# Projection and attention as one unrolled stage, by blocks of 512 queries

## The chip, the core and the metric

The kernel runs on one NeuronCore of a Trainium2 chip. The metric is device time in microseconds, the median of several executions. A profiled execution also gives the span from its first to its last instruction and a record of every instruction and DMA.

## What is computed

A transformer layer on 2 batches of 2048 tokens, width 256: a modulated layer norm, causal attention with 16 heads of 16 whose scores have three parts, and a feed-forward with 8 experts of which each token uses 2. Cut to what matters here:

```python
h = layernorm(x) * (1 + ca) + sa
q, k, v = split_heads(h @ qkv_w.T)                    # 16 heads of 16
scores = alpha * tanh(q k^T / beta)
soft, hexc = tanh(h @ hex_w.T), tanh(h @ q6_w.T)      # 6 codes each
scores += lam / 2 * soft soft^T                       # the same for all heads
scores += hexc M_head hexc^T / 6 * scale              # M_head is 6 x 6
out = softmax(causal(scores)) @ v
x = x + ga * (out @ out_w.T)
# then a layer norm, a router (top 2 of 8) and the experts; the change leaves these alone
```

## The kernel before

Five stages run one after the other, each with its own block of instruction streams for TensorE (PE), ScalarE (ACT), VectorE (DVE), GpSimd (POOL) and the DMA queue of SyncE (SP). No engine enters a stage before all have left the one before.

`stage_modulation` (L166) loads x whole, takes the statistics of its rows, computes the modulation rows, and ACT normalises x in place (L226 to L228).

`stage_projection` (L321) loops over eight blocks of 512 tokens. For each, POOL applies scale and shift (L431, L436), PE transposes the four tiles (L449) and multiplies: codes (L455), q and k in four groups of 128 rows (L461), the bilinear term (L466), v (L470), and a bound called guard (L476, L477). q, k, codes and bilinear term are split into two fp32r halves whose sum is the fp32 value; ACT and DVE do that. SP writes it all to scratch tensors in DRAM, with 23 DMAs a block (L392 to L415).

`stage_attention` (L550) loops over eight iterations, one for each batch and group of four heads. An iteration has 36 steps in a fixed order: for query block `qb` (0 to 3) of 512 queries, 4·qb full steps of 128 keys by 512 queries, then three diagonal steps, the last of which is 256 wide. A step has four parts. PE makes the raw scores of four heads (`raw_scores`, L669) in four PSUM banks that are not doubled, so it waits for the tanh of the step before. PE makes the bilinear scores of the four heads one after the other in two banks (`bilinear`, L681); each head waits for the sum of the head two before. PE multiplies the weights by v (`weighted_values`, L696). ACT does tanh (L734) and exp (L741), DVE the four sums (L771) and at the end of a query block the copy of the output (L779). POOL masks diagonal tiles (L654). PE runs raw scores three steps ahead: at step s it issues raw(s+3), bilinear(s+2) of heads 2 and 3, values(s), bilinear(s+3) of heads 0 and 1. All stationary operands of raw and bilinear scores have 128 rows, half of them zeros against the other head. Seven iterations are one loop body, the eighth is written out behind it. Loads (`load_block`, L581, 15 DMAs for each 512 keys) go into single buffers and wait until the iteration before has used them. With the first loads goes the load of x for the next stage (L625).

`stage_output` (L812) projects, adds x and takes statistics for 32 tiles; then come the router and the experts.

The lines that set the order on PE, and what SP does in the loop:

```python
for s in range(NSTEP):
    raw_scores(*at(s + PE_LEAD))
    bilinear(*at(s + PE_LEAD - 1), LAST_TWO)
    weighted_values(it, s)
    bilinear(*at(s + PE_LEAD), FIRST_TWO)
...
for qb in range(NBLK):
    if qb == NBLK - 1 and not last:
        for c in range(NBLK):
            load_block(sp, it + 1, c)
    store_out(sp, it, qb)
```

## Time and profile before

| | |
|---|---|
| time, median of 3 runs | 2195.11 us (2193.89 to 2205.54) |
| span of the profiled execution | 2187.8 us |
| PE busy / weight loads | 1909.5 us (87%) / 1097.2 us |
| ACT busy | 1282.9 us (59%) |
| DVE busy | 1300.8 us (59%) |
| POOL busy | 357.6 us (16%) |
| DMA | 172.28 MB in 139177 packets |

The profile is read by stage: busy shares of the whole span mix stages with different limits. In the timeline a row is a run of instructions of one kind: start, time from the first start to the last end, engine, line, tiles, count, and in brackets how long the engine was idle before it and what ended that. Ends of matmuls are modelled, and two ACT instructions in a row overlap in the records by some 0.15 us, so the distance from start to start is what one costs.

### The profile page before, as it was taken

Reading aid. Unit: us, or ns where it says so; the run is one execution under the profiler, and the core shown is the slowest. Engines: PE = TensorE matmul, PEld = TensorE weight load, DVE = VectorE, ACT = ScalarE, POOL = GpSimd, SP = SyncE. Lnnn points to the kernel's source line nnn. Section 1 sums busy time; section 2 is a strip of 40 time slices with the busy share of each in tenths; the row PEclk is TensorE's granted clock in tenths of the full one; section 3 lists DMA queues with packets and bytes.
Section 4 is the critical chain, followed back from the end, with each engine's and each line's share of the span. In section 5 each row is a group of like instructions: output and inputs, shape, how many; then the busy total and the mean of one; then the engine's idle time right before and its main releaser. Section 6 shows DMA issues by size and latency. Waiting matters only on the chain. (4 is left out here: it accounts for less than half of the span.)

```text
span 2187.8 us, 35435 instructions
## 1 busy us (share of the span) xinstructions
PE 1909.5 (87%) x9314; PEld 1097.2 (50%) x9315; DVE 1300.8 (59%) x2620; ACT 1282.9 (59%) x1387; POOL 357.6 (16%) x383
## 2 busy tenths in 40 slices
PE   2988199898999999989799996699089999999998
PEld 1433044444444444444344445588056667776665
DVE  5543177676877777777577774765234444444443
ACT  4323099898998989989799992244012222222222
POOL 1330200100001000000000003215501111111111
PEclk7988599999999999999899998899589999999999
DMA  3455661506033060521605204622262112222211
GB/s 122 153 171 199 152 152 43 107 10 125 23 71 82 19 130 5 101 52 40 108 5 101 53 6 127 200 116 79 89 190 34 32 31 34 34 34 34 34 31 25
DMA packets 139177, 172.28 MB, mean 79 GB/s; under 512 B 16672, under 2 KB 89248, under 8 KB 138976
## 3 DMA queue, kind: packets, MB, share of 16 engines
q1 hardware_dynamic: 116672, 143.00, 26.6%
q0 software_dynamic: 13824, 19.03, 5.0%
q10 hardware_dynamic: 8608, 9.47, 1.3%
q8 instruction: 22, 0.36, 0.1%
q14 instruction: 51, 0.42, 0.1%
HBM read 106.42 MB, written 65.03 MB: 78 GB/s over the span
## 5 line engine op out<-in xcount | busy, mean ns | idle before, releaser
L771 DVE SCALAR_TENSOR_TENSOR probs<-probs,scal,bil_ps 128x512 f32<-128x512 f32 (+1 forms) x1152 | 773.6, 715 | 278.5 <-ACT probs L734 169.6
L734 ACT ACTIVATE probs<-raw_ps 128x2048 f32<-128x2048 f32 (+1 forms) x288 | 518.7, 1801 | 84.3 <-PE raw_ps L669 84.3
L741 ACT ACTIVATE probs<-probs 128x2048 f32<-128x2048 f32 (+1 forms) x288 | 529.7, 1839 | 34.8 <-DVE probs L771 34.8
L681 PE MATMUL bil_ps<-u_mv,w_st 128*128 128x512 f32 (+3 forms) x1280 | 469.9, 426 | 54.1 <-DVE probs L771 30.8
L1442 ACT ACTIVATE hid_t<-h_tr_ps,b 128x128 f32<-128x128 f32 x576 | 156.3, 383 | 475.7 <-PE h_tr_ps L1406 409.6
L681 PEld LDWEIGHTS bil_ps<-u_mv,w_st 128*128 128x128 f32 x1280 | 217.3, 192 | 410.5 <-DVE probs L771 380.8
L669 PE MATMUL raw_ps<-q_mv,k_st 128*128 128x512 f32 (+3 forms) x1280 | 337.1, 390 | 52.8 <-DMA v_sb<-v_rows 45.1
L696 PE MATMUL o_ps<-probs,v_sb 128*32 128x512 f32 (+3 forms) x2560 | 298.5, 548 | 0.5 <-POOL probs L654 0.5
L669 PEld LDWEIGHTS raw_ps<-q_mv,k_st 128*128 128x128 f32 x1280 | 212.3, 194 | 143.9 <-ACT probs L734 70.1
L1397 PE MATMUL fc_ps<-w,rows_t 128*128 x576 | 262.1, 598 | 1.2 <-issue 0.6
L1417 PE MATMUL fc_ps<-w,hid_t 128*128 x1152 | 260.9, 380 | 1.7 <-DMA b<-in_b 0.9
L654 POOL TENSOR_SCALAR_AFFINE_SELECT probs<-probs 128x512 f32<-128x512 f32 x128 | 79.7, 635 | 982.5 <-ACT probs L741 982.5
L1417 PEld LDWEIGHTS fc_ps<-w,hid_t 128*128 128x128 f32 x1152 | 213.6, 190 | 28.2 <-issue 2.5
L1366 POOL DMA_INDIRECT out<-y,token x72 | 112.1, 1557 | 495.4 <-DVE y L1485 481.8
L1397 PEld LDWEIGHTS fc_ps<-w,rows_t 128*128 128x128 f32 x576 | 105.2, 193 | 107.0 <-issue 106.9
L1472 DVE COPY hid<-fc_ps 128x1024 f32<-128x1024 f32 x72 | 88.1, 1224 | 114.7 <-PE fc_ps L1397 114.7
L1481 DVE TENSOR_TENSOR y<-fc_ps,b 128x256 f32<-128x256 f32 x72 | 30.6, 424 | 204.7 <-PE fc_ps L1417 204.7
L696 PEld LDWEIGHTS o_ps<-probs,v_sb 128*32 128x32 f32 x2560 | 52.8, 109 | 66.9 <-ACT probs L741 36.4
L1406 PEld LDWEIGHTS h_tr_ps<-ident,hid 128*128 128x128 f32 x576 | 67.4, 141 | 37.5 <-issue 37.4
L1151 POOL DMA_INDIRECT x_rows<-rows_sb,place x64 | 62.6, 978 | 105.1 <-DVE place L1184 87.7
L1133 ACT ACTIVATE act_t<-hid_ps,rb 128x512 f32<-128x512 f32 x64 | 44.0, 689 | 60.7 <-PE hid_ps L1104 60.5
L1406 PE MATMUL h_tr_ps<-ident,hid 128*128 128x128 f32 x576 | 74.7, 273 | 0.0
(186 smaller groups left out, 1313.7 us busy)
## 6 DMA issues: line engine op xcount, KB each, us to landing
q_mv<-q_split SPq DMA_DIRECT2D x128, 128.0 KB
rows<-x_rows SPq DMA_DIRECT2D x72, 130.0 KB, 2.1
v_rows<-v_st SPq DMA_DIRECT2D x8, 1024.0 KB, 5.2
k_st<-k_split SPq DMA_DIRECT2D x64, 128.0 KB
k_st<-k_split SPq DMA_DIRECT2D x128, 64.0 KB
v_sb<-v_rows SPq DMA_DIRECT2D x32, 256.0 KB
o_t<-o_sb SPq DMA_DIRECT2D x32, 256.0 KB, 2.2
o_t_sb<-o_t SPq DMA_DIRECT2D x32, 256.0 KB, 2.8
```

Source lines behind the costliest of these rows:

```text
L669: mm = pe.matmul(raw_ps[:, hd, column:column + width], k_st[:, hd // 2, kt * P:(kt + 1) * P], q_mv[:, hd, qb * BLK + query:qb * BLK + quer ...
L681: mm = pe.matmul(bil_ps[:, hd % 2, column:column + width], w_st[:, kt * P:(kt + 1) * P], u_mv[:, hd, qb * BLK + query:qb * BLK + query + w ...
L696: mm = pe.matmul(o_ps[hd * VW:(hd + 1) * VW, query:query + width], v_sb[:, kt, hd * VW:(hd + 1) * VW], probs[:, s % NBUF, hd, column:colum ...
L734: act.activation(probs[:, s % NBUF, :, first:BLK], raw_ps[:, :, first:BLK], ACT.Tanh).then_inc(tanh_ready, 1)
L741: act.activation(scores, scores, ACT.Exp).then_inc(exp_ready, 1)
L771: dve.scalar_tensor_tensor(scores, scores, scal[:, ALPHA:ALPHA + 1], bil_ps[:, hd % 2, first:BLK], ALU.mult, ALU.add).then_inc(sum_ready, 1)
L1366: pool.indirect_dma_start(out, bass.IndirectOffsetOnAxis(ap=token[:, u:u + 1], axis=0), y[:, u % 2, :], None, compute_op=ALU.add).then_inc ...
L1397: mm = pe.matmul(fc1_ps[:, half * BLK:(half + 1) * BLK], rows_t[:, p, k * P:(k + 1) * P], w1[:, ds(e * (KC * HID) + (k * HID + half * BLK) ...
L1406: tr = pe.transpose(h_tr_ps[:, hc * P:(hc + 1) * P], hid[:, p, hc * P:(hc + 1) * P], ident[:, :])
L1417: mm = pe.matmul(fc2_ps[:, 0:D], hid_t[:, p, hc * P:(hc + 1) * P], w2[:, ds(e * (HC * D) + hc * D, D)], start=(hc == 0), stop=(hc == HC - 1))
L1442: silu = act.activation(hid_t[:, p, cols], h_tr_ps[:, cols], ACT.Silu, bias=b1[:, ds(e * HC + hc, 1)])
L1472: dve.tensor_copy(hid[:, p, :], fc1_ps[:, :]).then_inc(hid_ready, 1)
```

## The change

Projection and attention become one stage, `stage_front`, without loops. The unit of order is a block of 512 queries of one batch; the eight blocks come as (batch 0, queries 0), (batch 1, queries 0), (batch 0, queries 1) and so on, each with four iterations for the four groups of heads. So there are 32 iterations of 3, 7, 11 or 15 steps and 288 steps as before. Keys, queries, bilinear operands and values of an iteration have two buffers each; an iteration loads the keys and values of all query blocks up to its own.

The projection of a block is cut into eleven parts: two transposes (T0, T1), codes (C), q and k (Q0 to Q3), bilinear term (L), v (V0, V1), guard (G). Blocks 0 and 1 are projected ahead of attention (all but G of block 1), with five PSUM banks in turn. For the six others one part stands behind `weighted_values` in each of eleven steps in a row, beginning where block i−2 begins its attention; these parts use one bank, `part_ps`. DVE empties that bank between heads 1 and 2 of its sums one step later; POOL splits three steps later, after that step's mask; SP stores four steps later. The halves of q and k, codes and bilinear term come from POOL instead of ACT and DVE (for blocks 0 and 1 those of q and k still come from ACT and DVE).

ACT no longer normalises all of x; x is loaded again by blocks, and DVE (block 0 and 1) or POOL normalises it. Raw and bilinear scores use stationary operands of 64 and 50 rows, heads 0 and 2 in the lower half of the array's rows, heads 1 and 3 in the upper half. The load of x for `stage_output` moves to that stage, ahead of its first loads of `o_t`.

```diff
+assert TPB == 4
+BLOCKS = [(i % B, i // B) for i in range(N_BLK)]
+ITERS = [(i, g) for i in range(N_BLK) for g in range(NG)]
...
+STEPS = [(it, pieces) for it, (i, _) in enumerate(ITERS) for pieces in block_steps(BLOCKS[i][1])]
 NSTEP = len(STEPS)
-LAST_OF = {qb: max(s for s, (q, _) in enumerate(STEPS) if q == qb) for qb in range(NBLK)}
-FIRST_OF = {qb: min(s for s, (q, _) in enumerate(STEPS) if q == qb) for qb in range(NBLK)}
...
+DIAG = [s for it in range(len(ITERS)) for s in range(LAST[it] - 2, LAST[it] + 1)]
+MASKS_BEFORE = {s: n for n, s in enumerate(DIAG)}
...
+PARTS = ["T0", "T1", "C", "Q0", "L", "Q1", "Q2", "V0", "Q3", "V1", "G"]
+EARLY = 2
+START = {i: FIRST[i * NG] for i in range(N_BLK)}
+HEAD_PARTS = ([(0, o) for o in PARTS[:-1]] + [(1, o) for o in ("T0", "T1", "C")] + [(0, "G")]
+              + [(1, o) for o in PARTS[3:-1]])
+SLOT = {START[0]: (1, "G")}
+SLOT.update({START[i - EARLY] + (i == EARLY) + n: (i, o) for i in range(EARLY, N_BLK) for n, o in enumerate(PARTS)})
+PART_ORDER = HEAD_PARTS + [SLOT[s] for s in sorted(SLOT)]
+PART_NUMBER = {part: n for n, part in enumerate(PART_ORDER)}
+EMPTIED = {part: sum(o != "C" for _, o in PART_ORDER[:n + 1]) for n, part in enumerate(PART_ORDER)}
+POOL_LAG = 3
+NORM_AT = {START[i - EARLY - 1] + 4 + 2 * t: (i, t) for i in range(EARLY + 1, N_BLK) for t in range(TPB)}
+STORE_AT = {s + POOL_LAG + 1: part for s, part in SLOT.items()}
+KEYS_AT = {max(LAST[it - 2] - PE_LEAD, 0): it for it in range(2, len(ITERS))}
+BIAS_AT = {LAST[it - 2] - PE_LEAD + 1: it for it in range(2, len(ITERS))}
+VALUES_AT = {LAST[it - 2] + 1: it for it in range(2, len(ITERS))}
+CODES_AT = {LAST[i * NG - 2] - PE_LEAD - 1: i for i in range(1, N_BLK)}
+ROWS_AT = {FIRST[(i - EARLY - 2) * NG + 2]: i for i in range(EARLY + 2, N_BLK)}
...
-            stage_modulation(nc, a, modrow, ident, scal, x_sb, stats, rstd, lattice)
-            stage_projection(nc, a, dram, modrow, ident, scal, x_sb, lattice)
+            stage_modulation(nc, a, modrow, ident, scal, shift, rstd, lattice)
+            stage_front(nc, a, dram, modrow, ident, scal, shift, rstd, lattice)
...
-            act.wait_ge(shift_ready, 1)
-            for n in range(NTILE):
-                tile = x_sb[:, n * D:(n + 1) * D]
-                act.activation(tile, tile, ACT.Identity, bias=shift[:, n:n + 1], scale=rstd[:, n:n + 1])
...
+        k_st = sb("k_st", [P, 2, HG // 2, T], F32R)
+        q_mv = sb("q_mv", [P, 2, HG // 2, BLK], F32R)
+        w_st = sb("w_st", [P, B, T], F32R)
+        u_mv = sb("u_mv", [P, 2, HG // 2, BLK], F32R)
+        v_sb = sb("v_sb", [P, 2, T // P, HG * VW])
+        probs = sb("probs", [P, NBUF, HG, BLK])
+        o_sb = sb("o_sb", [P, 2, BLK])
...
+        part_ps = ps("part_ps", [P, BLK])
...
+            def load_keys(it):
+                i, g = ITERS[it]
+                c, p = BLOCKS[i][1], it % 2
+                if it >= 2:
+                    sp.wait_ge(raw_mm, LAST[it - 2] + 1)
+                for m in range(2):
+                    sp.wait_ge(st_qk[m], 32 * N_QK * (i + 1))
+                seen, own = slice(0, (c + 1) * BLK), slice(c * BLK, (c + 1) * BLK)
+                k_both = heads("k_split", 2 * HD, i, g, seen).rearrange("(j z r) t -> z r j t", z=2, r=2 * HD)
+                q_rows = heads("q_split", 2 * HD, i, g, own).rearrange("(j z r) t -> z r j t", z=2, r=2 * HD)
+                load = lambda dst, src: sp.dma_start(dst.bitcast(F32), src).then_inc(keys_in[p], 16)
+                for z in range(2):
+                    row = z * ROWS
+                    load(k_st[row:row + 2 * HD, p, :, seen], k_both[z])
+                    load(k_st[row + 2 * HD:row + 3 * HD, p, :, seen], k_rows[z, 1])
+                    load(k_st[row + 3 * HD:row + 4 * HD, p, :, seen], k_rows[z, 0])
+                    for half in range(2):
+                        load(q_mv[row + half * 2 * HD:row + (half + 1) * 2 * HD, p, :, :], q_rows[z])
...
+            load_rows(0)
+            load_rows(1)
+            for o in PARTS[:-1]:
+                store(0, o)
+            load_keys(0)
+            sp.wait_ge(pad_ready, 1)
+            load_codes(0)
+            load_values(0)
+            load_rows(2)
+            store(0, "G")
+            load_bias(0)
+            load_keys(1)
+            load_bias(1)
+            load_values(1)
+            load_rows(3)
+            for o in PARTS[:-1]:
+                store(1, o)
+            for s in range(NSTEP):
+                if s in CODES_AT:
+                    load_codes(CODES_AT[s])
+                if s in KEYS_AT:
+                    load_keys(KEYS_AT[s])
+                if s in BIAS_AT:
+                    load_bias(BIAS_AT[s])
+                if s in VALUES_AT:
+                    load_values(VALUES_AT[s])
+                if s in STORE_AT:
+                    store(*STORE_AT[s])
+                if s in ROWS_AT:
+                    load_rows(ROWS_AT[s])
+                if s - 1 in LAST:
+                    store_out(LAST.index(s - 1))
+            store_out(len(ITERS) - 1)
...
+            def split_heads(i, m):
+                pool.wait_ge(emptied, EMPTIED[i, f"Q{m}"])
+                pool.wait_ge(st_qk[m % 2], 16 * N_QK * (2 * i + m // 2))
+                then_wait(pool.tensor_copy(qk_hi[:, m % 2, :], qk_f[:, m % 2, :]))
+                pool.tensor_tensor(qk_lo[:, m % 2, :], qk_f[:, m % 2, :], qk_hi[:, m % 2, :].bitcast(F32),
+                                   ALU.subtract).then_inc(lo_ready, 1)
+                pool.wait_ge(lo_ready, 4 * (i - EARLY) + m + 1)
...
+            for s in range(NSTEP):
+                if s in MASKS_BEFORE:
+                    mask(s)
+                if s - POOL_LAG in SLOT:
+                    i, o = SLOT[s - POOL_LAG]
+                    if o == "C":
+                        split_codes(i)
+                    elif o == "L":
+                        split_lattice(i)
+                    elif o == "G":
+                        split_guard(i)
+                    elif o[0] == "Q":
+                        split_heads(i, int(o[1]))
+                if s in NORM_AT:
+                    normalise(pool, then_wait, *NORM_AT[s])
...
+            def project(i, o):
+                bank = bank_of((i, o))
+                emptied_before(pe, (i, o))
+                if o[0] == "T":
+                    k = int(o[1])
+                    for t in range(TPB):
+                        pe.wait_ge(h_ready, TPB * i + t + 1)
+                        mm = pe.transpose(bank[:, t * P:(t + 1) * P], h[:, t, k * P:(k + 1) * P], ident[:, :])
+                elif o == "C":
+                    pe.wait_ge(emptied, EMPTIED[i, "T1"])
+                    for k in range(KC):
+                        mm = pe.matmul(bank[0:HROWS, :], wcode[:, k, :], h_t[:, k, :],
+                                       start=(k == 0), stop=(k == KC - 1))
+                elif o[0] == "Q":
+                    m = int(o[1])
+                    for k in range(KC):
+                        mm = pe.matmul(bank, wqkv[:, k, m * P:(m + 1) * P], h_t[:, k, :],
...
+                        row = hd % 2 * ROWS
                         mm = pe.matmul(raw_ps[:, hd, column:column + width],
-                                       k_st[:, hd // 2, kt * P:(kt + 1) * P],
-                                       q_mv[:, hd, qb * BLK + query:qb * BLK + query + width],
-                                       start=True, stop=True)
...
+                for hd in pair:
+                    row = hd % 2 * ROWS
+                    if HG * s + hd >= 2:
+                        pe.wait_ge(sum_ready, HG * s + hd - 1)
                     for kt, column, query, width in pieces:
-                        mm = pe.matmul(bil_ps[:, hd % 2, column:column + width], w_st[:, kt * P:(kt + 1) * P],
-                                       u_mv[:, hd, qb * BLK + query:qb * BLK + query + width],
+                        mm = pe.matmul(bil_ps[:, hd % 2, column:column + width],
+                                       w_st[row:row + BIAS_ROWS, b, kt * P:(kt + 1) * P],
+                                       u_mv[row:row + BIAS_ROWS, p, hd // 2, query:query + width],
                                        start=True, stop=True)
...
+            pe.wait_ge(p_in, 64)
+            for i, o in HEAD_PARTS:
+                project(i, o)
+            pe.wait_ge(emptied, EMPTIED[HEAD_PARTS[-1]])
...
+            for s in range(NSTEP):
+                if s + PE_LEAD < NSTEP:
+                    raw_scores(s + PE_LEAD)
+                if s + PE_LEAD - 1 < NSTEP:
+                    bilinear(s + PE_LEAD - 1, LAST_TWO)
+                weighted_values(s)
+                if s in SLOT:
+                    project(*SLOT[s])
+                if s + PE_LEAD < NSTEP:
+                    bilinear(s + PE_LEAD, FIRST_TWO)
...
+                if s - 2 in SLOT and SLOT[s - 2][1] == "C":
+                    make_codes(SLOT[s - 2][0])
+                exp(s)
...
+            for t in range(TPB):
+                normalise(dve, then_wait, 0, t)
+            dve.memset(w_st[:, :, :].bitcast(F32), 1.0).then_inc(pad_ready, 1)
+            dve.memset(v_st[:, :, :, HD:VW], 1.0).then_inc(ones_ready, 1)
+            for n, (i, o) in enumerate(HEAD_PARTS):
+                if o != "C":
+                    empty(i, o)
+                if i == 0 and o[0] == "Q":
+                    normalise(dve, then_wait, 1, int(o[1]))
...
+            for s in range(NSTEP):
+                for hd in range(HG):
+                    if hd == HG // 2 and s - 1 in SLOT and SLOT[s - 1][1] != "C":
+                        empty(*SLOT[s - 1])
+                    if s + DVE_LEAD < NSTEP:
+                        score_sum(s + DVE_LEAD, hd)
+                if s in LAST:
+                    evacuate(LAST.index(s))
...
             sp.dma_start(token_f[:, :], a["token_rows"]).then_inc(t_in, 16)
+            sp.dma_start(rows_sb[:, :].rearrange("p (n d) -> p n d", d=PAY)[:, :, 0:D],
+                         a["x"].rearrange("(n p) d -> p n d", p=P)).then_inc(x_back, 16)
             for m in range(OB):
```

## Rows read from the trace of the kernel before

**Rows 1.** Busy time by stage: us and count of PE, PEld, DVE, ACT, POOL; clock, DMA share, GB/s

```profile
0.00:44.40 44.40, 12.28 (x24) 5.14 (x25) 30.30 (x123) 20.66 (x41) 0.20 (x4) 0.84 0.39 132
44.40:244.30 199.90, 148.14 (x400) 63.64 (x400) 82.83 (x113) 56.12 (x80) 51.45 (x64) 0.84 0.50 170
...
268.00:1321.00 1053.00, 990.78 (x5116) 477.81 (x5115) 791.35 (x1183) 982.10 (x576) 79.70 (x128) 0.97 0.32 65
```

**Rows 2.** Timeline of SP in projection: first issue of two blocks in a row

```profile
173.81 0.75 SPq L392 DMA_DIRECT2D code_split<-w_hi  x1
...
196.28 0.74 SPq L392 DMA_DIRECT2D code_split<-w_hi  x1
```

**Rows 3.** Timeline of one full step of attention

```profile
901.68 2.81 DVE L771 SCALAR_TENSOR_TENSOR probs<-probs,scal,bil_ps 128x512 f32<-128x512 f32 x4 [0.76 <-ACT probs L734]
...
903.14 0.19 PEld L681 LDWEIGHTS bil_ps<-u_mv,w_st 128*128 128x128 f32 x1 [0.47 <-DVE probs L771]
903.20 1.93 ACT L734 ACTIVATE probs<-raw_ps 128x2048 f32<-128x2048 f32 x1
...
903.57 1.07 PE L696 MATMUL o_ps<-probs,v_sb 128*32 128x512 f32 x8
...
906.76 1.94 ACT L734 ACTIVATE probs<-raw_ps 128x2048 f32<-128x2048 f32 x1
```

**Rows 4.** Groups by form in attention: busy us, mean ns, idle before

```profile
L734 ACT ACTIVATE probs<-raw_ps 128x1024 f32<-128x1024 f32 x32 | 34.0, 1063 | 0.0
```

**Rows 5.** Timeline at returns of the loop: first return, then the sixth

```profile
412.35 1.06 ACT L741 ACTIVATE probs<-probs 128x1024 f32<-128x1024 f32 x1 [3.85 <-DVE probs L771]
...
1068.14 0.88 DVE L771 SCALAR_TENSOR_TENSOR probs<-probs,scal,bil_ps 128x256 f32<-128x256 f32 x2 [6.21 <-issue]
...
1084.80 1.88 ACT L734 ACTIVATE probs<-raw_ps 128x2048 f32<-128x2048 f32 x1 [2.04 <-PE raw_ps L669]
```

**Rows 6.** Timeline: end of modulation, a memset, the first tanh

```profile
38.78 0.42 DVE L317 SCALAR_TENSOR_TENSOR modrow<-gate_sign,gate_abs 128x256 f32<-128x256 f32 x1
...
247.09 1.76 DVE L761 MEMSET w_st<- 64x2048 f32 x1 [0.48 <-issue]
...
268.00 1.88 ACT L734 ACTIVATE probs<-raw_ps 128x2048 f32<-128x2048 f32 x1 [49.33 <-PE raw_ps L669]
```

**Rows 7.** Timeline of POOL at the start of stage_output

```profile
1339.27 1.89 POOL L931 CAST rw_hi<-rw 128x2048 fp32r<-128x2048 f32 x1 [14.12 <-DMA tile_first<-in_iota]
1341.24 4.51 POOL L933 TENSOR_TENSOR rw_lo<-rw,rw_hi 128x2048 fp32r<-128x2048 f32 x1
1345.71 0.72 POOL L938 TENSOR_TENSOR rows_sb<-rows_sb,gated 128x256 f32 x1
```

**Rows 8.** Timeline of SP: one load_block, first and last issue

```profile
248.97 1.29 SPq L584 DMA_DIRECT2D k_st<-k_split  x3
...
255.10 0.50 SPq L606 DMA_DIRECT2D v_sb<-v_rows  x1
```

**Rows 9.** Waits of ACT from 300 to 405 us: total, times, longest

```profile
ACT probs L734 <- PE raw_ps L669: 1.5, 3, 0.6
```

**Rows 10.** Busy time while the first loads of attention run

```profile
249.00:289.00 40.00, 20.98 (x84) 13.37 (x84) 12.65 (x20) 15.91 (x10) 11.88 (x10) 0.58 1.01 160
```

**Rows 11.** One block of projection: busy time, and two of PE's rows

```profile
71.10:88.90 17.80, 16.61 (x51) 7.53 (x50) 11.15 (x14) 6.96 (x10) 6.90 (x8) 1.00 0.58 204
...
71.19 1.10 PE L449 MATMUL tv_ps<-ident,h 128*128 128x128 f32 x8
...
75.28 7.13 PE L461 MATMUL qk_ps<-h_t,wqkv 128*128 128x512 f32 x16
```

**Rows 12.** Two lines of DVE: ns min/median/max, first and last start

```profile
L517 DVE TENSOR_TENSOR w_lo<-code,w_hi x8: 671/673/1203, 59.7 to 207.6; 12x512 fp32r<-12x512 f32 x8
L527 DVE SCALAR_TENSOR_TENSOR qk_lo<-qk_ps,scal,qk_hi x16: 729/732/753, 61.8 to 211.2; 128x512 fp32r<-128x512 f32 x16
```

**Rows 13.** DMA issues of the page: count, KB, us from issue to landing

```profile
out<-rows_sb SPq DMA_DIRECT2D x1, 4096.0 KB, 14.4
```

More of the change, by code:

```diff
@@ L738, in exp @@
                 first = first_column(s)
[L739 removed]
+                act.wait_ge(sum_ready, HG * (s + 1))
                 scores = probs[:, s % NBUF, :, first:BLK]
                 act.activation(scores, scores, ACT.Exp).then_inc(exp_ready, 1)
[L743 to L751 removed]
```

705 lines of the change are left out of this document (345 added, 360 removed).

## The prediction

> **What bounds the kernel now.** I read the busy time by stage first. Projection lasts 200 us, attention from its first tanh at 268 on 1053 [rows 1], 24 us lie between, and 867 are left for all behind it. In projection no engine is near full: PE is busy for 148 of 200 us, ACT for 56. There SP sets the pace. It issues 23 stores for a block without waiting for an engine; those of one begin at 173.81, those of the next at 196.28, so 22.4 us a block [rows 2]. Attention is set by ACT: in a full step tanh follows tanh after 3.56 us (903.20 to 906.76) with nothing between them but the exp [rows 3]. Of 288 tanh, 32 are half as wide and take 1.06 us [rows 4], and so do 32 exp. With full steps at 3.56 and half ones at some 2.0, that is 256·3.56 + 32·2.0 = 975 us; the stage took 1053. Of the 78 us between, 44 lie where the loop goes back: 14 gaps of ACT around six returns, of which the first and the last are shown. Behind each stands DVE, idle for up to 6.2 us on "issue", which waited for nothing but its own instructions [rows 5]. Some 6 lie at the start, the rest in small gaps at ends of query blocks.
>
> PE is busy for 991 of 1053 us, but its rows show that it waits inside the step: a head's bilinear product follows the sum of two heads before [rows 3]. So it has room by throughput and little by order. That decides what a part costs.
>
> **The change part by part**, against the span of 2187.8 us.
>
> *The time to the first tanh.* Before it is 268.0. After, modulation ends with DVE at 39.2 [rows 6] instead of with ACT's normalising at 44 [rows 1]. Block 0: x lands and DVE normalises four tiles, until 48; two memsets, of which that of `w_st` is twice 1.76 [rows 6], until 53; transposes, their copies and codes until 58. Splitting codes is now POOL's. A copy of 128x2048 took it 1.89 us and an operation with two inputs 4.51, so 0.5 and 1.15 for 512 columns [rows 7]: the first store at 61. From there SP is the chain: its queue is in order. To be issued ahead of the last part of block 1 are block 0's stores (18 us: the 22.4 above without most of the gaps between issues, which come from register work), keys, bias, values and codes twice (a load of 15 DMAs took 6.6 us; an iteration now has 17 and an output, so 8) [rows 8], and block 1's stores up to Q1, some 11: 47 us. Behind these stand waits that nothing hides: Q2 and Q3 reuse the buffer of Q0 and Q1 and wait for their stores to land, `load_keys` waits for q and k, `load_values` for v, `load_bias` for the guard, which has POOL in its chain; about 3 us each, 15 to 17 in all. 61 + 47 + 16 + one raw score makes 125. Bounds: 110 if the waits overlap, 140 if each is doubled. Gain 143.
>
> *The loop.* Without a jump the 44 us at the returns go. That code met for the first time costs nothing itself shows in the first pass: from 300 us to the first return ACT waits for raw scores three times, 0.6 us at most [rows 9]. Gain 44; bounds 0 and 44. The start keeps its 6.
> The Trainium skill, page "Runtime: NRT & Kernel Launch", section "Instruction fetch mechanics", says that fetching ahead is sequential and a taken branch breaks it. The trace agrees: the stalls stand at the returns only.
>
> *The first 24 steps.* Blocks 0 and 1 have only diagonal steps, three to an iteration: ACT needs 2·3.56 + 2.0 = 9.1 us, 73 for eight. In that time come the loads of eight iterations and the stores of blocks 2 and 3. SP: 8·8.5 + 2·18 = 104 us. DMA: an iteration moves some 2.1 MB. While such loads ran, the share was full, and 160 GB/s for 40 us are 6.4 MB [rows 10], so 13 us for an iteration; I take 10 to 13, for the first part of these 40 us was memsets. The stores of a block took half the engines for 22.4 us [rows 1, 2], so 11. Together 102 to 126 us. POOL: for a block splits of codes 6.2, bilinear 3.7, q and k 7.8, guard 2.5 and normalising 10.4 make 31, twice, and 24 steps with masks 20: 82 us. The 22 parts on PE (below) hide under the same time. I take 120 for the 24 steps, 47 more than ACT needs. Bounds 103 (ACT with the parts alone) and 160 (SP and transfers one after the other).
>
> *The parts of blocks 4 to 7.* From one block's first transpose to its last product PE is busy for 16.6 us; q and k take 7.13 of these, 1.8 for each part, and eight transposes 1.10 [rows 11]. A part stands between values and the bilinear product of the next step. From the start of ACT's free raw score on, the order in a step is: sums of heads 0 and 1 (1.5), bilinear of head 3 (0.43), values (1.07), the part, bilinear of heads 0 and 1 (0.4, by the 0.43 of one): 3.4 plus the part [rows 3]. Only 0.1 to 0.2 of 3.56 is free. So the part lies nearly whole on the path: 15.5 us a block, 62 for four. DVE's copy of a bank, as long as a sum of the same shape (0.70), falls in the longer period, for DVE is idle 0.76 in each step [rows 3]. Bounds: 4 us a block if PE had its order free (1.2 us of each step), 27 if the copy and two drains come on top: 16 to 108.
> The Trainium skill, page "TensorEngine Tiling (Array Packing)", section "Key Properties", says that changing the tiling mode drains PE. Each part changes it once more. Here values follow a bilinear product 0.43 us after its weight load [rows 3], and the load itself is 0.19 of it, so a drain beside the product is small: I estimate 0.1 to 0.2 for each part by the rule, 5 to 9 us in sum.
>
> *Halves of the array.* With 64 rows the four raw scores go in pairs, if the two halves run together as the four column groups of values do (eight products, of the kind of which q and k need sixteen in 7.13 us [rows 11], in 1.07 us [rows 3]). In a full step ACT hides it. At ends of query blocks raw scores are late by up to 0.6 [rows 9]; I take 5 us of gain, bounds 0 and 15.
>
> *POOL and the mask.* Values of step s come 3.8 us after exp(s) in the steady order, so a mask may be 3 us late for nothing. Splitting codes takes 6.2, once a block: 1 us each, in the rounding. POOL beside DVE: the sum with one input from PSUM is the same kind as L527, which never exceeded 0.753, while L517 with both inputs in SBUF went from 0.67 to 1.20 in some of its eight, under POOL [rows 12]. The sums stay as they are. ACT's tanh of codes falls where it waits.
>
> *The tail.* x for `stage_output` was loaded at the beginning of attention. Now its 4 MB stand ahead of `o_t` and `rw1`; 4 MB of the same tile, on the way out, landed in 14.4 us [rows 13]. POOL splits `rw1` ahead of its first sum at 1345.71 [rows 7], and all of that moves by the transfer: +14, bounds 8 and 22.
>
> Sum: −143 −44 +47 +62 −5 +14 = −69, so 2119 us of span. The runs lie 7 above the span (2195.1 to 2187.8): 2126 us.
>
> **The rivals.**
> *A, slower.* Every iteration begins with a wait for its keys. SP has one queue, and there the loads of an iteration stand behind stores that wait for POOL, which waits for masks of steps to come; keys released by raw(LAST) have four steps to be issued and land. For it: SP's 104 us against 73 in the first steps. Against: iterations of 7 to 15 steps last 23 to 53 us, and their loads take 8.5 us of SP and 12 to 25 of DMA. Its place is the 24 iterations of blocks 2 to 7; from 3.3 us each on it eats the gain. With 5 to 6 us each: 2126 + 130 = 2256.
> *B, the parts are cheap.* PE's room by throughput is used, and raw scores in pairs open more. Then 62 becomes 16 to 25: 2126 − 41 = 2085. Against it is the order in the step.
> *C, the early steps are dear.* SP, transfers and POOL add up instead of overlapping: 160 instead of 120, and parts with copy and drains, +10 to 15: 2178.
> *D, straight code stalls too*, since DVE, PE and SP fetch all of it through the busy DMA engines: +44, 2170. The first pass, during which loads ran, speaks against it. By the rule of the Trainium skill's page "Runtime: NRT & Kernel Launch" it would not happen either.
>
> **How the numbers follow.** Forecast 0.52, A 0.10, B 0.16, C 0.15, D 0.07. The likeliest gives 2126. The range takes B's 2085 with the earlier bound of the first tanh (−12), and C and D with 7 us over, and leaves out A and the far ends: 2072 to 2185. A measurement of this kernel can tell about 0.5%, 11 us, from no change. Faster by over 11 us (below 2184): the forecast, B, D and most of C, 0.84. Within: the rest of C and a light form of A, 0.06. Slower: 0.10.
>
> **What would show it.** First tanh between 110 and 140, with SP's queue packed before it. Steps 0 to 23 in about 120 us, ACT waiting for raw scores there and these for keys. In steps with a part of q, tanh to tanh about 5.2 us; in those with a transpose under 4; in all others 3.56. No gap of DVE on "issue" over 2 us. The first sum of POOL in `stage_output` 14 us later after the end of attention than the 25 of before. I am wrong if steps with parts cost under 4.2 (B), if iterations of blocks 2 to 7 begin with gaps over 3 us (A), or if the first tanh lies beyond 150.

## The result, and the profile after

The changed kernel takes 2234.8 us (median of 4 runs, 2222.1 to 2247.4) where the kernel before takes 2194.5 on the same chip: ratio 1.018, 95% interval 1.012 to 1.025. It is slower by 40 us, 1.8%. The forecast was 2126, with the range up to 2185. The profiled execution has a span of 2238.5 us.

The page of the changed kernel: busy time of PE, then the 40 slices of PE and of the granted clock, and the two groups of products that now read half of the rows (busy, mean ns; idle before).

```profile
PE 1905.1 (85%) x9314; PEld 984.6 (44%) x9315; DVE 1271.2 (57%) x2611; ACT 1240.1 (55%) x1292; POOL 519.4 (23%) x543
...
PE   2658999999898899988888884789359999999998
...
PEclk7759898877878867799999997899679999999999
...
L763 PE MATMUL bil_ps<-u_mv,w_st 50*128 50x512 f32 (+3 forms) x1280 | 482.0, 521 | 106.6 <-DVE probs L903 93.9
...
L746 PE MATMUL raw_ps<-q_mv,k_st 64*128 64x512 f32 (+3 forms) x1280 | 218.7, 430 | 36.1 <-DVE v_st L888 26.6
```

A slice is 56 us. In slices 5 to 17, where parts lie between the steps, PEclk shows mostly 7 and 8 while PE is busy for eight or nine tenths. Before, the clock of the attention was 0.97 [rows 1].

Busy time of the changed kernel by stretch (us; us and count of PE, PEld, DVE, ACT, POOL; granted clock, DMA share, GB/s). The stretches are the first 24 steps (blocks 0 and 1), the steps of blocks 2 to 5, those of blocks 6 and 7 (beside which nothing is projected), and all that follows.

```profile
133.70:254.50 120.80, 108.19 (x570) 48.94 (x568) 71.52 (x118) 75.65 (x49) 76.57 (x90) 0.83 0.74 182
254.50:912.50 658.00, 595.41 (x2778) 225.12 (x2779) 418.46 (x638) 507.99 (x293) 170.12 (x198) 0.79 0.54 115
912.50:1350.70 438.20, 387.52 (x2053) 137.88 (x2052) 328.28 (x490) 419.83 (x242) 20.47 (x33) 0.91 0.40 70
1350.70:2238.50 887.80, 761.32 (x3798) 549.54 (x3794) 393.00 (x1199) 224.22 (x692) 213.46 (x182) 0.93 0.29 74
```

Where the forecast failed can be read from the sum of these. It had 125 + 120 us up to step 24, and they are 133.7 + 120.8. It had 993 us for blocks 2 to 7, and they are 658.0 + 438.2 = 1096.2. It had 881 behind, and they are 887.8. Nearly the whole error, 103 of 119 us, lies in blocks 2 to 7.

Two things are to be seen there. The first shows best where no part lies. One iteration of block 7 (15 steps), cut into its first steps up to 1141.2, the 9.3 us behind them, and the rest:

```profile
1131.10:1141.20 10.10, 8.61 (x56) 3.34 (x55) 8.08 (x13) 9.94 (x7) 1.85 (x3) 0.95 1.06 157
1141.20:1150.50 9.30, 9.19 (x33) 2.96 (x32) 5.07 (x8) 7.53 (x6) 0.00 (x0) 0.50 1.05 196
1150.50:1160.70 10.20, 8.61 (x48) 3.02 (x48) 7.97 (x12) 10.09 (x6) 0.00 (x0) 1.00 0.10 30
1160.70:1185.70 25.00, 21.91 (x122) 7.91 (x122) 19.78 (x31) 24.84 (x15) 0.64 (x1) 1.00 0.13 27
```

At 0.50, the level of 1.2 GHz, PE is the bound (9.19 of 9.30 us), ACT waits, and the two steps in it last 4.3 and 5.0 us, not 3.56 [rows 3]. Ahead of the fall PE worked 8.61 of 10.10 us, with products on half of the rows. In each of the eight iterations of blocks 6 and 7 the clock is lowered once, for 10.2 us, and they take 54.6 to 55.3 us; the iterations' stretches of 15 steps in the kernel before take 52.7 us (the last 53.2) with no fall.

The second: eight single steps of 7.0 to 12.0 us from tanh to tanh, three of them over 9. The longest, in block 4, as SP, POOL and PE show it (start, duration, engine; in brackets the idle time before and what ended it).

```profile
567.90 0.64 SPq L476 DMA_DIRECT2D q_split<-qk_hi  x1
568.59 0.60 SPq L476 DMA_DIRECT2D q_split<-qk_lo  x1
...
581.87 0.61 POOL L653 CAST qk_hi<-qk_f 128x512 fp32r<-128x512 f32 x1 [12.42 <-DMA q_split<-qk_lo]
582.56 1.27 POOL L654 TENSOR_TENSOR qk_lo<-qk_f,qk_hi 128x512 fp32r<-128x512 f32 x1
583.90 0.64 POOL L673 TENSOR_SCALAR_AFFINE_SELECT probs<-probs 128x512 f32<-128x512 f32 x1
...
584.59 1.08 PE L782 MATMUL o_ps<-probs,v_sb 128*32 128x256 f32 x8 [4.28 <-POOL probs L673]
```

POOL's split of Q2 reuses the buffer of Q0 and waits for its store, issued at 567.90 and 568.59: the split starts at 581.87, 13 us after the second issue. The mask of a diagonal step stands behind it in POOL's order and comes at 583.90; PE's values wait 4.28 us for the mask, and all steps behind them with PE. Over the whole kernel (us in all, times, longest):

```profile
POOL qk_hi L653 <- DMA q_split<-qk_lo: 49.8, 8, 12.4
...
ACT probs L830 <- PE raw_ps L746: 113.5, 106, 7.2
ACT probs L837 <- DVE probs L903: 85.2, 124, 2.2
...
ACT qk_hi L822 <- DMA q_split<-qk_lo: 47.0, 4, 25.4
```

### The profile page after: what moved, and what is told of

The parts are those of the page before. It is cut to its first block and busy times, and to the rows that moved or that the text cites. A ratio compares the mean times of both kernels' runs of the same rounds, so it can differ in the third digit from the quotient of the medians.

```text
span 2238.5 us, 31048 instructions
## 1 busy us (share of the span) xinstructions
PE 1905.1 (85%) x9314; PEld 984.6 (44%) x9315; DVE 1271.2 (57%) x2611; ACT 1240.1 (55%) x1292; POOL 519.4 (23%) x543
## 5 line engine op out<-in xcount | busy, mean ns | idle before, releaser
L830 ACT ACTIVATE probs<-raw_ps 128x2048 f32<-128x2048 f32 (+1 forms) x288 | 513.0, 1781 | 113.8 <-PE raw_ps L746 113.5
L763 PE MATMUL bil_ps<-u_mv,w_st 50*128 50x512 f32 (+3 forms) x1280 | 482.0, 521 | 106.6 <-DVE probs L903 93.9
L837 ACT ACTIVATE probs<-probs 128x2048 f32<-128x2048 f32 (+1 forms) x288 | 523.8, 1819 | 86.7 <-DVE probs L903 85.2
L763 PEld LDWEIGHTS bil_ps<-u_mv,w_st 50*128 50x128 f32 x1280 | 197.1, 208 | 588.5 <-DVE probs L903 507.7
L782 PE MATMUL o_ps<-probs,v_sb 128*32 128x512 f32 (+3 forms) x2560 | 356.3, 644 | 10.1 <-POOL probs L673 10.1
L746 PE MATMUL raw_ps<-q_mv,k_st 64*128 64x512 f32 (+3 forms) x1280 | 218.7, 430 | 36.1 <-DVE v_st L888 26.6
L746 PEld LDWEIGHTS raw_ps<-q_mv,k_st 64*128 64x128 f32 x1280 | 128.3, 221 | 65.8 <-DVE v_st L888 27.0
```

The source lines that it names most:

```text
L746: mm = pe.matmul(raw_ps[:, hd, column:column + width], k_st[row:row + ROWS, p, hd // 2, kt * P:(kt + 1) * P], q_mv[row:row + ROWS, p, hd / ...
L763: mm = pe.matmul(bil_ps[:, hd % 2, column:column + width], w_st[row:row + BIAS_ROWS, b, kt * P:(kt + 1) * P], u_mv[row:row + BIAS_ROWS, p, ...
L782: mm = pe.matmul(o_ps[hd * VW:(hd + 1) * VW, query:query + width], v_sb[:, p, kt, hd * VW:(hd + 1) * VW], probs[:, s % NBUF, hd, column:co ...
L830: act.activation(probs[:, s % NBUF, :, first:BLK], raw_ps[:, :, first:BLK], ACT.Tanh).then_inc(tanh_ready, 1)
L837: act.activation(scores, scores, ACT.Exp).then_inc(exp_ready, 1)
```

## The experiments

Theory 1 was that the halves of the array lower the granted clock, and that this is most of what is missing; the waits for stores are the next piece. Theory 2 put the clock down to the parts and the unequal steps that come with them. Ratios are to the kernel before, run on the same chip, with 95% intervals. The four stretches of the profiled executions, in us:

| kernel | first tanh | steps 0 to 23 | blocks 2 to 7 | behind | span |
|---|---|---|---|---|---|
| forecast | 125 | 120 | 993 | 881 | 2119 |
| changed | 133.7 | 120.8 | 1096.2 | 887.8 | 2238.5 |
| a_fullrows | 135.6 | 112.8 | 1005.0 | 887.7 | 2141.1 |
| a_bilfull | 135.5 | 114.3 | 1003.2 | 891.5 | 2144.4 |
| a_qk4 | 100.9 | 139.2 | 1062.5 | 889.0 | 2191.6 |
| a_both | 107.8 | 130.2 | 984.3 | 890.8 | 2113.1 |
| a_late | 106.5 | 131.4 | 976.7 | 891.4 | 2106.1 |

**Halves of the array in the kernel before (b_halves).** Beside the products, the loads of the bias rows and codes go to both halves.

```diff
-  k_st[:, hd // 2, kt * P:(kt + 1) * P],
-  q_mv[:, hd, qb * BLK + query:qb * BLK + query + width],
+  k_st[hd % 2 * ROWS:(hd % 2 + 1) * ROWS, hd // 2, kt * P:(kt + 1) * P],
+  q_mv[hd % 2 * ROWS:(hd % 2 + 1) * ROWS, hd, qb * BLK + query:qb * BLK + query + width],
...
-  w_st[:, kt * P:(kt + 1) * P],
-  u_mv[:, hd, qb * BLK + query:qb * BLK + query + width],
+  w_st[hd % 2 * ROWS:hd % 2 * ROWS + BIAS_ROWS, kt * P:(kt + 1) * P],
+  u_mv[hd % 2 * ROWS:hd % 2 * ROWS + BIAS_ROWS, hd, qb * BLK + query:qb * BLK + query + width],
```

> The kernel before with the array halves alone: raw products of an even head read rows 0 to 63 of stationary and moving operand, of an odd head rows 64 to 127, bilinear products the same with 50 rows; the order, the loops and the projection stage stay (four more small loads per block of keys, in cover). Theory 1 (products on half of the rows make the chip grant the 1.2 GHz level for stretches, and this is the missing term): the steps of 3.42 us go to the 3.6 to 3.7 us that the last two blocks of the changed kernel show, so the eight iterations grow by 3 to 5%, 30 to 55 us; time 2225 to 2250 us, and the granted clock of the stretch 268 to 1321 us falls from near 1.0 to 0.85 to 0.9. Theory 2 (the slow clock of the changed kernel comes from its parts and its unequal steps, the halves are harmless): 2180 to 2195 us, clock of the attention unchanged. My prediction's term said 0 to -15 us (its value was -5).

Measured: 2290.6 us, ratio 1.040 (1.034 to 1.046), so 88 us lost: more than theory 1 had said, and no theory without the halves allows it. The attention of this kernel, as a window (columns as above):

```profile
268.00:1415.00 1147.00, 1023.47 (x5090) 381.25 (x5090) 784.33 (x1183) 998.47 (x576) 78.86 (x127) 0.79 0.29 62
```

The clock is 0.79 where it was 0.97 [rows 1], with no part, no unrolling and the same order of work. The added loads are not the reason: b_halves_bil below has them too and keeps 0.94.

**All rows in the changed kernel (a_fullrows).**

```diff
-  k_st[row:row + ROWS, p, hd // 2, kt * P:(kt + 1) * P],
-  q_mv[row:row + ROWS, p, hd // 2, query:query + width], start=True, stop=True)
+  k_st[:, p, hd // 2, kt * P:(kt + 1) * P],
+  q_mv[:, p, hd // 2, query:query + width], start=True, stop=True)
...
-  w_st[row:row + BIAS_ROWS, b, kt * P:(kt + 1) * P],
-  u_mv[row:row + BIAS_ROWS, p, hd // 2, query:query + width],
+  w_st[:, b, kt * P:(kt + 1) * P],
+  u_mv[:, p, hd // 2, query:query + width],
```

> The changed kernel with all 128 rows in every raw and bilinear product (same count, order and columns; the two heads of a pair are then summed in each, so its scores are other numbers; one memset of u_mv on GpSimd ahead of block 0's codes, 4 to 10 us, mostly in cover). Theory 1: the granted clock in the attention rises from 0.72-0.92 to over 0.95, the last two blocks go from 438 us to 422 us or less, the whole from 2235 to 2150-2180 us. Theory 2: the clock stays as low; the products no longer run in pairs, and the time stays at 2235 or grows to 2260 us.

Measured: 2144.0 us, ratio 0.976 (0.973 to 0.980): 91 us come back by the number of rows alone. The same cut through an iteration of block 7 as above:

```profile
1042.70:1052.80 10.10, 9.72 (x56) 4.69 (x55) 8.22 (x14) 9.77 (x7) 1.85 (x3) 1.00 1.07 155
1052.80:1062.10 9.30, 9.27 (x44) 3.71 (x44) 7.12 (x11) 9.30 (x7) 0.00 (x0) 1.00 1.02 174
1062.10:1072.30 10.20, 10.19 (x47) 4.41 (x48) 8.35 (x12) 10.20 (x6) 0.00 (x0) 1.00 0.18 53
1072.30:1097.30 25.00, 24.66 (x123) 11.44 (x123) 18.82 (x29) 24.84 (x16) 1.85 (x3) 1.00 0.21 37
```

The loads run beside it as before (DMA share 1.07 and 1.02), so they are not what lowers the clock. The iteration takes 52.5 us.

**Rows in work or busy time (b_rows64).** In the kernel before all raw products read rows 0 to 63, all bilinear ones rows 0 to 49; none can run beside another.

```diff
-  k_st[:, hd // 2, kt * P:(kt + 1) * P],
-  q_mv[:, hd, qb * BLK + query:qb * BLK + query + width],
+  k_st[0:ROWS, hd // 2, kt * P:(kt + 1) * P],
+  q_mv[0:ROWS, hd, qb * BLK + query:qb * BLK + query + width],
...
-  w_st[:, kt * P:(kt + 1) * P],
-  u_mv[:, hd, qb * BLK + query:qb * BLK + query + width],
+  w_st[0:BIAS_ROWS, kt * P:(kt + 1) * P],
+  u_mv[0:BIAS_ROWS, hd, qb * BLK + query:qb * BLK + query + width],
```

> The kernel before with all raw products on rows 0 to 63 and all bilinear ones on rows 0 to 49, for the odd heads too (their raw scores are then zero, so the result is another): half of the rows are in work, but no two products can run beside one another, so TensorE is busy as long as before. Theory 1a (rows in work set the clock): a fall of the granted clock to 0.85-0.9 and 2240 to 2290 us as with the halves. Theory 1b (TensorE's busy time sets it, and the halves lower it because the pairs run beside one another): clock near 1.0 and 2190 to 2205 us.

Measured: 2703.1 us, ratio 1.235 (1.229 to 1.241), far beyond both numbers. Its attention:

```profile
268.00:1821.00 1553.00, 1542.65 (x5062) 807.38 (x5060) 790.82 (x1175) 1009.79 (x572) 77.17 (x124) 0.50 0.21 44
```

PE is busy for 1542.65 of 1553 us and the clock is 0.50 throughout: steps of 5.6 us, bound by PE at 1.2 GHz. Both kernels enter attention partly at the lower level. The same 37 us soon after, in the kernel before and then here:

```profile
293.00:330.00 37.00, 35.72 (x184) 17.30 (x184) 29.18 (x44) 36.34 (x23) 2.49 (x4) 1.00 0.45 132
```

```profile
293.00:330.00 37.00, 37.00 (x129) 20.10 (x128) 18.91 (x30) 23.95 (x15) 2.49 (x4) 0.50 0.45 127
```

PE is busy for 35.72 us and has the full clock, or for all 37.00 and does not get it. So busy time doesn't hold the clock; how many of the array's rows the products (and their weight loads, which shrink with them) use does. Theory 1b is out. That pairs which overlap lose less than products one by one (1.040 against 1.235) fits the same reading, though no run tests it alone: in a pair both halves work at once.

The Trainium skill, page "TensorE: Matmul & The Clock Gate", section "What's actually happening", says that the gate between the two levels goes by how busy PE has been. Taken as busy time, the trace here contradicts it: 99% busy at the lower level. And the Trainium skill's page "TensorEngine Tiling (Array Packing)", section "When to Use Tiling", recommends row tiling for a contraction of up to 64; here it cost 4.0% when both kinds were tiled: the clock fell, and since ACT was the bound the shorter products bought nothing.

**Which of the two kinds (b_halves_raw, b_halves_bil, a_bilfull).** The diff of b_halves cut in two, and its counterpart in the changed kernel (only the bilinear lines of a_fullrows' diff).

> Of the kernel before with the array halves (2290.56 us, ratio 1.040), only the raw products on half of the rows; the bilinear ones read all 128 rows again. If what counts is how many rows of the array are in work on average, the loss is about half: 2235 to 2250 us. If the clock falls only once both kinds are halved (a bound that one alone doesn't pass): 2190 to 2205 us. If the raw ones alone do it (four products that end in 0.7 us in place of 1.2): 2275 to 2290 us.

> The counterpart: only the bilinear products on half of the rows (50 of them), the raw ones on all 128. Each pair of bilinear products waits for VectorE's sums, so little time is shared between the two. By rows in work: 2235 to 2250 us. By a bound that one alone doesn't pass: 2190 to 2205 us. If the pairs' shorter time is what counts, nothing: 2190 to 2205 us.

> The changed kernel with all 128 rows in the bilinear products alone (each then sums the bias of two heads, so its scores are other numbers; the raw products keep their halves). In the kernel before, halves of the raw products alone cost nothing (ratio 0.998), halves of the bilinear ones 0.7%, both 4.0%. If that holds in the changed kernel, this one edit gives back nearly all that all rows gave (2235 to 2144 us): 2140 to 2155 us, granted clock of 256 to 1253 us at 0.97 or more. If the unequal steps of the changed kernel need the raw ones whole too: 2170 to 2200 us.

Measured: raw halves alone 2181.2 us, ratio 0.998 (0.995 to 1.001), nothing lost or gained; bilinear halves alone 2204.3, ratio 1.007 (1.004 to 1.010); together they had cost 1.040. The losses don't add up. Raw halves alone are the case that the forecast had priced, and its −5 us fits them. Of the three outcomes named ahead, the one by which one alone passes hardly costs anything is the nearest, though the bilinear ones aren't free. The attention of the first and of the second:

```profile
268.00:1310.00 1042.00, 947.93 (x5088) 363.44 (x5084) 778.11 (x1182) 982.37 (x575) 77.86 (x125) 0.97 0.32 66
```

```profile
268.00:1330.00 1062.00, 1019.82 (x5054) 472.72 (x5058) 785.89 (x1174) 978.32 (x572) 77.21 (x124) 0.94 0.32 67
```

In the changed kernel, whole bilinear products alone (a_bilfull) give 2146.3 us, ratio 0.976 (0.973 to 0.978), the same as all rows. So the edit to take back is one of the two.

**The loop alone (b_unrolled).**

```diff
-            with dve.Fori(0, NIT - 1) as it:
+            for it in range(NIT - 1):
                 iteration(it, False)
```

and the same for the other four engines.

> The kernel before with the loops over the eight iterations of its attention written out, nothing else. The prediction's term: the seven returns cost 6.3 us each, so -44 us: 2145 to 2155 us, with no fall of the granted clock where the returns were. Theory 2 in its second form (straight code makes the engines wait for instructions, which the changed kernel's 55 fetches on one queue would show): 2180 us or more. Rival: only the part of a return in which VectorE waits for nothing else is saved, 4 us each: 2165 us.

Measured: 2150.4 us, ratio 0.9795 (0.976 to 0.983), so 45 us gained where the term said 44. The stretch from 268 to 1270 has a clock of 0.99:

```profile
268.00:1270.00 1002.00, 980.61 (x5080) 468.32 (x5080) 787.24 (x1179) 977.09 (x574) 77.98 (x125) 0.99 0.34 69
```

**Store waits (a_qk4).**

```diff
-        qk_hi = sb("qk_hi", [P, 2, BLK], F32R)
-        qk_lo = sb("qk_lo", [P, 2, BLK], F32R)
+        qk_hi = sb("qk_hi", [P, 4, BLK], F32R)
+        qk_lo = sb("qk_lo", [P, 4, BLK], F32R)
...
-                pool.wait_ge(st_qk[m % 2], 16 * N_QK * (2 * i + m // 2))
+                pool.wait_ge(st_qk[m], 16 * N_QK * i)
...
-                if 2 * i + m // 2:
-                    act.wait_ge(st_qk[m % 2], 16 * N_QK * (2 * i + m // 2))
+                if i:
+                    act.wait_ge(st_qk[m], 16 * N_QK * i)
```

> The changed kernel with four buffers for the halves of q and k, so GpSimd's split of a part waits for a store of the block before, not for one issued a few steps ago (the normalise steps use the x tile in place to make room). What the trace says: six long steps of 7.0 to 12.0 us, in which a mask stood behind such a wait, cost about 35 us, and ScalarE waited 47 us for these stores at the start: -30 to -45 us, 2190 to 2205 us. If these waits only took the place of others (the clock, the parts): -0 to -10 us.

Measured: 2193.7 us, ratio 0.996 (0.994 to 0.999), 41 us less than the changed kernel by the medians and 47 by the profiled executions. The table shows where. The first tanh comes 33 us earlier, but the 24 steps behind it take 18 more, at a clock of 0.77 for 0.83; whether it is the clock, the loads or the stores that holds them isn't shown. The rest, 34 us, is in blocks 2 to 7. The waits of ACT and POOL for `q_split<-qk_lo` are gone from its table of waits, and the three steps over 9 us (9.2, 12.0 and 11.0) take 5.3, 4.9 and 4.9: 17 us. Four steps of 6.9 to 8.4 us remain. The other 17 us come with a clock that is lowered less, why isn't shown. Blocks 2 to 7 of the changed kernel, then of a_qk4:

```profile
254.50:1350.70 1096.20, 982.93 (x4826) 363.00 (x4826) 746.74 (x1127) 927.82 (x533) 190.59 (x231) 0.84 0.48 97
```

```profile
240.09:1302.60 1062.51, 950.38 (x4826) 354.63 (x4826) 745.31 (x1127) 925.05 (x532) 188.66 (x230) 0.87 0.49 100
```

**The load of x (b_xmoved).** The one `dma_start` of `rows_sb` moved from `stage_attention` to `stage_output`, behind `token_rows`.

> The kernel before with the load of x for the residual moved from the attention stage to the head of the output stage, where the changed kernel has it. My term for the tail was +14 us (8 to 22), and the changed kernel's tail came out 20 us longer: 2205 to 2215 us if the load is all of it; 2195 to 2202 us if half of the 20 us comes with the straight code (the tail of the kernel with written-out loops was 6 us longer).

Measured: 2196.3 us, ratio 1.0035 (1.0006 to 1.0065): 1 to 14 us, with 11.7 us more behind the attention in the profile (880.7 for 869.0). In the changed kernel DVE shows what it waits for, and PE:

```profile
1356.87 0.28 DVE L1081 MEMSET blank<- 128x260 f32 x1 [3.03 <-PEq L340]
1373.21 0.15 DVE L1085 COPY blank<-token_f 128x1 f32<-128x1 f32 x1 [16.07 <-DMA rows_sb<-in_x]
1375.31 0.26 DVE L1093 RECIPROCAL rden<-o_tr_ps 128x16 f32<-128x16 f32 x1 [1.94 <-PE o_tr_ps L1029]
...
PE o_tr_ps L1029 <- DMA o_t_sb<-o_t: 23.6, 2, 21.1
```

Its `stage_output` begins its first tile 12.2 us later after the end of attention than that of before; b_xmoved 12.1. The loops-only kernel has 6 us more behind the attention as well (875.0 for 869.0), with the start of the output stage unmoved. The trace of b_unrolled shows where: in the router, where ACT stands idle on "issue", waiting for nothing that the profile shows. The longest such wait, then all of them (us, times, longest):

```profile
1480.46 0.69 ACT L1133 ACTIVATE act_t<-hid_ps,rb 128x512 f32<-128x512 f32 x1 [6.40 <-issue]
...
ACT act_t L1133 <- issue: 9.7, 6, 6.4
```

The changed kernel shows the same (9.7 us in 6 waits, 6.3 the longest) and the kernel before none. But b_halves, whose loops stay, has it too (9.1 in 5, 6.4; 874.6 us behind the attention), so it isn't the written-out loops that bring it; what does stays open. With the 12 of x it makes up 18 of the 18.8 us of the changed kernel (887.8 for 869.0).

**A version from these findings (a_both).** Half rows for the raw products alone; bilinear ones on all rows, with `u_mv` for four heads and zeros below row 50; four buffers for q and k; keys and bias of iteration 2 ahead of block 1's stores; x behind the first tiles of `o_t`.

```diff
-        u_mv = sb("u_mv", [P, 2, HG // 2, BLK], F32R)
+        u_mv = sb("u_mv", [P, 2, HG, BLK], F32R)
...
-                                       w_st[row:row + BIAS_ROWS, b, kt * P:(kt + 1) * P],
-                                       u_mv[row:row + BIAS_ROWS, p, hd // 2, query:query + width],
+                                       w_st[:, b, kt * P:(kt + 1) * P],
+                                       u_mv[:, p, hd, query:query + width],
...
             load_rows(3)
+            load_keys(2)
             for o in PARTS[:-1]:
                 store(1, o)
+                if o == "L":
+                    load_bias(2)
```

> The changed kernel mended at the places that the runs have named, the result unchanged: bilinear products on all 128 rows with zeroed other rows (u_mv for all four heads, one load per kind), four buffers for q and k halves, the keys and bias of iteration 2 loaded ahead of block 1's stores, and x loaded behind the first tiles of o_t. Sum: first tanh 101 us; the first 24 steps 125 to 139 us in place of 139; blocks 2 to 5 at the clock of 2.4 GHz 489 us and 62 for the parts; blocks 6 and 7 421 us; tail 875 to 885 us: 2070 to 2095 us, 0.945 to 0.955 of the time before. If the gains overlap (the store waits were hidden behind the slow clock, or the clock still falls): 2100 to 2140 us.

Measured: 2115.6 us, ratio 0.962 (0.960 to 0.964). That is 20 us above the upper end of its sum. Blocks 2 to 7 take 984.3 us for the 972 of the sum, the first tanh comes 7 us later than in a_qk4, and the tail (890.8) is not shorter: with x behind the tiles the first tile starts at once, but DVE's first products then wait 20.3 us for POOL's sum, which waits for x. The stage by two windows, blocks 2 to 5, then 6 and 7:

```profile
238.00:802.70 564.70, 533.05 (x2774) 211.98 (x2774) 414.90 (x637) 498.96 (x292) 169.71 (x197) 1.00 0.62 134
802.70:1222.30 419.60, 394.16 (x2053) 143.02 (x2052) 327.47 (x490) 416.43 (x242) 20.51 (x33) 1.00 0.43 73
```

With the clock at 1.00 and one long step only, this kernel gives the price of the parts by itself. Against 23.4 us for an iteration of 7 steps and 37.7 for one of 11 (full steps at 3.57, two half ones together 2.0), blocks 3, 4 and 5 show 15.5, 15.8 and 15.8 us over in the two iterations beside which parts lie. Block 2 shows 25.1; one of its steps takes 8.6. There PE's values start at 256.70, as the load of `v_sb` issued at 243.91 has landed.

**The order within a step (a_late).** On top of a_both:

```diff
-                if s in SLOT:
-                    project(*SLOT[s])
                 if s + PE_LEAD < NSTEP:
                     bilinear(s + PE_LEAD, FIRST_TWO)
+                if s in SLOT:
+                    project(*SLOT[s])
```

> The mended kernel (2115.6 us, ratio 0.962, its parts at 15.5 to 15.8 us a block) with each part put behind the first two bilinear products of its step and not ahead of them. My prediction took the period of a step with a part as TensorE's own 3.4 us plus the part, whatever the order. If that holds: blocks 3 to 5 stay at 15 to 16 us over, the whole within 5 us, ratio 0.960 to 0.965. Rival: the period comes from the chain part, bilinear product, VectorE's sum, exp, and the order matters: 3 to 6 us less a block, ratio 0.950 to 0.957; or more, where the raw scores that follow now wait behind the part and with them the tanh: up to 10 us more.

Measured: 2106.9 us, ratio 0.958 (0.956 to 0.961), the fastest of all. Blocks 4 and 5 go from 15.8 to 12.6 and 12.5 us over, the low end of what the rival had said; the ratio lies between the two that were named. Block 3 stays (15.6): one of its steps takes 7.8, with PE's values 1.82 us behind a mask that stands behind POOL's splits of codes. The kernels ran on different chips, and 0.962 (0.960 to 0.964) against 0.958 touch in their intervals, so the time within the blocks is the firmer sign. PE in one step with a part of v, of a_both, then of a_late:

```profile
521.37 1.07 PE L781 MATMUL o_ps<-probs,v_sb 128*32 128x128 f32 x16
522.37 1.99 PE L727 MATMUL part_ps<-wqkv,h_t 128*128 128x256 f32 x8
524.02 0.81 PE L762 MATMUL bil_ps<-u_mv,w_st 128*128 128x512 f32 x2
524.76 0.73 PE L746 MATMUL raw_ps<-q_mv,k_st 64*128 64x512 f32 x4
525.50 0.51 PE L762 MATMUL bil_ps<-u_mv,w_st 128*128 128x512 f32 x1
526.16 0.50 PE L762 MATMUL bil_ps<-u_mv,w_st 128*128 128x512 f32 x1 [0.15 <-DVE probs L902]
```

```profile
517.37 1.07 PE L781 MATMUL o_ps<-probs,v_sb 128*32 128x128 f32 x16
518.37 0.84 PE L762 MATMUL bil_ps<-u_mv,w_st 128*128 128x512 f32 x2
519.05 1.89 PE L727 MATMUL part_ps<-wqkv,h_t 128*128 128x256 f32 x8
520.87 0.73 PE L746 MATMUL raw_ps<-q_mv,k_st 64*128 64x512 f32 x4
521.53 0.73 PE L762 MATMUL bil_ps<-u_mv,w_st 128*128 128x512 f32 x2
522.19 0.64 PE L781 MATMUL o_ps<-probs,v_sb 128*32 128x256 f32 x8
```

Values to values: 5.22 us in the first (521.37 to 526.59), 4.82 in the second. In both PE hardly pauses: in the second DVE has its bilinear product 1.6 us earlier, and then PE does the part. Steps with a part of q or k in the same stretch take 5.21 to 5.31 in a_both and 4.71 to 4.91 in a_late. So a part still lies nearly whole on PE; the order is worth some 0.4 us a step.

## Why the prediction was wrong, step by step

**Halves of the array: the step that failed.** It said "In a full step ACT hides it" and gave −5 us, bounds 0 and −15. The mechanism that it named is there: four half-row raw products go in 0.63 to 0.73 us, not 1.2, and ACT hides them. What it never asked is what such products do to the granted clock. It had no upper bound above zero, though nothing in the trace of before shows a product on half of the rows in steady state. In its place the runs put +91 us (changed against a_fullrows), and +88 when the edit is made alone (b_halves). None of the four rivals held this; no number of the prediction moves with the clock at all. Raw halves alone would have kept to the term (b_halves_raw, −0.2%); it is both kinds together that fail it.

**POOL and the mask: the second step.** It counted the time of each of POOL's operations and the slack of 3 us behind an exp, and put their sum "in the rounding". But POOL's queue also holds waits: the split of Q2 and Q3 waits for the store of Q0 and Q1 to land, 49.8 us in eight waits, with masks behind. The same buffers are named in the paragraph on the first tanh, and only there. a_qk4 gets 34 us back in blocks 2 to 7, half of them in the three longest steps, the rest beside a clock that is lowered less. Beside whole rows the same three steps take 13.3, 12.4 and 13.0 us in a_fullrows and 5.3, 4.9 and 4.9 in a_both: 24 us, of which 5 go again to the wait for `v_sb`.

**The parts of blocks 4 to 7: right, to the size, in three blocks of four.** 15.5 us a block were forecast, with a step of q at 5.2 us; a_both shows 15.5 to 15.8, and 5.21 to 5.31. The fourth takes 25.1 with its wait for `v_sb`. The late order shows that 3 us of the 15.5 are order and not PE's work, so the reading "only 0.1 to 0.2 is free" was a little too strict. Rival B (4 us a block) is out.

**The loop: right.** −44 forecast, −45 measured alone. Rival D, stalls in straight code, is out: DVE's waits on "issue", 6.21 us at one return in [rows 5], don't appear among its waits in the new stage. (ACT's 9.7 us on "issue" in the router lie behind it.)

**The first tanh and the first 24 steps: right in sum, in part by luck.** 133.7 against 125, within its bounds of 110 to 140, and 120.8 against 120. But the waits that nothing hides were put at 15 to 17 us, and ACT alone waits 47.0 us for stores of q, 25.4 the longest. Four buffers bring the first tanh to 100.9, so the rest of that term was too large. And a_fullrows does the 24 steps in 112.8 us, with a clock of 0.98 where the changed kernel has 0.83: 8 of the 120.8 came with the clock. a_qk4 adds that the two terms belong together: what the first tanh gains by shorter waits is half given back by the steps behind (139.2). The 160 of rival C were not seen.

**The tail: somewhat small.** +14 forecast, +18.8 measured: 12 by the load of x (b_xmoved), for which 14 were forecast, and 6 in the router, for which the prediction had no term; b_halves has them too, so the loops are not what brings them.

**Rival A** had the right sign by another mechanism. But for the one wait for `v_sb`, SP waits in the new stage for PE and not the other way round; iterations of blocks 6 and 7 begin with no gap for keys.

For blocks 2 to 7 the rows of the table give 1096.2 − 91.2 (rows of the array) − 20.7 (long steps, and the other small edits of a_both) = 984.3, against 993 forecast. That is nearer than the terms were. The 993 holds 902 us of ACT's steps, 62 for parts, 34 of small gaps taken over from before and −5; a_both shows 72 for parts and leaves 10 for gaps. So +10 and −24 offset each other in part.

## What to carry to other kernels

A product that uses fewer rows is not always free where another engine hides its time: read the granted clock in the stretch behind the edit, and ask of every edit that makes TensorE's products smaller what share of the array stays in work. When work moves onto an in-order queue, list its waits and what stands behind each, not its durations alone; a buffer reused within a few steps makes a store's landing part of the step. And price unlike edits alone, one in each kernel: here −143 (−134 measured), −44 and 15.5 a block were nearly met, the first with two misses inside it, and one small edit turned the sum.

## What the runs showed of the hardware that was not expected

- TensorE 99% busy for 1553 us at a granted clock of 0.50 (1.2 GHz), with all raw products on 64 and all bilinear ones on 50 rows (b_rows64), while values used all rows in 32 columns. With 128 rows in the same order the clock is 0.97 to 0.99. Rows that hold zeros count: in the raw products of the kernel before half of the moving rows are zeros (0.97), in those of a_fullrows none are (0.99 over blocks 2 to 7).
- The losses of two kinds of half-row products don't add: −0.2% and +0.7% alone, +4.0% together. What share of the array, over what time, decides isn't settled by these runs.
- Half-row products in pairs do run at once: four in 0.63 to 0.73 us for 1.2, and 1.05 for them at the lower level.
- A full load of the DMA engines (share 1.07) beside whole-row products left the clock at 1.00.
